# Product-key attention: SyncE fetches three sets of rows a head by byte offset instead of two by row number

## What is computed

```python
kv_scores, indices = _pk(x, Wq_pk, pk_keys)              # 16 scores and row numbers of each token and head
ind = indices + offsets[None, None, :, None]             # + head * 16384
k = jnp.einsum('bnhk,bnhkd->bnhd', kv_scores, keys_table[ind])
v = jnp.einsum('bnhk,bnhkd->bnhd', kv_scores, values_table[ind])
# causal attention of q over k, v within a head, then @ Wo, summed over the heads
```

## Time and profile before

| | us |
|---|---|
| median of three runs | 10244.51 |
| lowest, highest | 10216.51, 10246.37 |
| the profiled execution | 10217.74 |
| its span, first to last instruction | 10215.9 |
| POOL busy in the span | 7665.5 (75%) |
| VectorE busy | 6964.4 (68%) |
| TensorE matmul, weight load busy | 5480.3, 4291.3 |
| ScalarE busy | 2991.9 |

### The profile page before, as it was taken

One profiled execution on the slowest core, in us unless ns is written; L12 is line 12 of the kernel. 1 busy time (PEld: TensorE's weight loads), 2 busy tenths in 40 slices (PEclk: granted clock), 3 DMA queues, 4 the chain that ended last, 5 costly groups with the idle time before them and its releaser, 6 DMA issues.

```text
span 10215.9 us, 172728 instructions
## 1 busy us (share of the span) xinstructions
PE 5480.3 (54%) x23108; PEld 4291.3 (42%) x23108; DVE 6964.4 (68%) x42588; ACT 2991.9 (29%) x9770; POOL 7665.5 (75%) x8083
## 2 busy tenths in 40 slices
PE   5655555555555555555555555555555555555555
PEld 4444444444444444444444444444444444444343
DVE  8866666666766667666666666766667676666663
ACT  4322232222322223223232222322223222222222
POOL 5777777777777777777777777777777777777776
PEclk7877777777777777777777777777777777777777
DMA  3333333333333333333333333333333333333333
GB/s 109 104 107 107 107 111 107 107 107 107 111 107 107 107 107 111 107 107 107 107 111 107 107 107 109 109 107 107 107 109 109 107 107 107 108 108 107 107 107 99
DMA packets 458936, 1097.67 MB, mean 107 GB/s; under 512 B 164737, under 2 KB 198529, under 8 KB 457793
## 3 DMA queue, kind: packets, MB, share of 16 engines
q0 software_dynamic: 387168, 1057.74, 36.0%
q1 hardware_dynamic: 70752, 31.47, 1.2%
HBM read 1084.36 MB, written 4.19 MB: 107 GB/s over the span
## 4 chain that ended last, share of the span: by engine, by line
POOL 74%; issue 24%; DVE 1%; PE 1%; POOLq 0%; DMA 0%; ACT 0%; SPq 0%; DVEq 0%; ACTq 0%
POOL ring L325 74%; DVE hot L947 0%; DMA wo<-in_Wo 0%; POOLq L340 0%; POOLq L338 0%; PE ps_w L605 0%; PE ps_o L658 0%; PE ps_s L682 0%; DVE nmax L994 0%; DVE ps_v L869 0%; POOLq L339 0%; DMA ring<-in_table,idx 0%; POOLq L336 0%; DVE sidx L895 0%; DVE left L893 0%
## 5 line engine op out<-in xcount | busy, mean ns | idle before, releaser
L325 POOL DMA_INDIRECT ring<-in_table,idx x8066 | 7664.0, 950 | 2524.4 <-issue 2457.5
L605 PE MATMUL ps_w<-ring,diag 128*128 128x256 f32 x8192 | 2987.0, 544 | 4103.0 <-DMA ring<-in_table,idx 4103.0
L605 PEld LDWEIGHTS ps_w<-ring,diag 128*128 128x128 f32 x8192 | 2298.2, 288 | 4688.3 <-issue 4101.3
L947 DVE SCALAR_TENSOR_TENSOR hot<-rank,posf,cand 128x54 f32<-128x54 f32 x8192 | 1661.0, 272 | 0.3
L866 DVE TENSOR_SCALAR ps_v<-ring,wgt 128x256 f32<-128x256 f32 x512 | 248.8, 486 | 1928.4 <-DMA ring<-in_table,idx 1928.4
L869 DVE SCALAR_TENSOR_TENSOR ps_v<-ring,wgt,ps_v 128x256 f32<-128x256 f32 x3072 | 1478.3, 481 | 19.6
L432 ACT COPY probT<-ps_p 128x512 f32<-128x512 f32 (+3 forms) x768 | 342.4, 480 | 3909.5 <-PE ps_p L649 3897.4
L415 ACT ACTIVATE diag<-ident,wgt 128x128 f32<-128x128 f32 x4096 | 1253.3, 395 | 1.9 <-PE ps_w L605 1.9
L424 ACT ACTIVATE prob<-ps_s,nmax 128x128 f32<-128x128 f32 (+7 forms) x512 | 378.9, 740 | 2000.3 <-DVE nmax L994 2000.3
L880 DVE TENSOR_TENSOR kv<-part,ps_w 128x256 f32<-128x256 f32 x512 | 215.8, 422 | 841.6 <-PE ps_w L605 500.7
L947 DVE DVE_READ_ACCUMULATOR hot<-rank,posf,cand 128x1 f32 x8192 | 661.8, 81 | 0.0
(11 more groups left out here) (118 smaller groups left out, 7016.7 us busy)
## 6 DMA issues: line engine op xcount, KB each, us to landing
far<-in_table SPq DMA_DIRECT2D x16128, 1.0 KB
ring<-in_table,idx POOLq DMA_INDIRECT x8066
xin<-in_x SPq DMA_DIRECT2D x8, 512.0 KB, 4.6
mask<-in_adj SPq DMA_DIRECT2D x1, 4096.0 KB, 14.5
out_x<-acc SPq DMA_DIRECT2D x64, 64.0 KB
far_idx<-idx SPq DMA_DIRECT2D x126, 0.5 KB
ring<-in_WqpkT SPq DMA_DIRECT2D x1, 512.0 KB, 16.5
ring<-in_keysT SPq DMA_DIRECT2D x1, 512.0 KB, 18.5
```

The source lines that it names most:

```text
L325: pool.indirect_dma_start(out=ring[:, t % RING, k, :], out_offset=None, in_=table, in_offset=bass.IndirectOffsetOnAxis(ap=idx[:, t, k:k + ...
L605: ins = nc.tensor.matmul(pw_ps, diag[:, k, :], ring[:, t % RING, k, :], start=(k == 0), stop=(k == PE_ROWS - 1))
L947: c = step(nc.vector.scalar_tensor_tensor(out=hot[:, k, :], in0=rank[:], scalar=posf[:, k:k + 1], in1=cand[:, 1, :], op0=ALU.is_equal, op1 ...
```

## The change

`FAR` becomes (2, 5, 7): three sets a head are fetched by SP, and POOL issues 125 gathers a head instead of 126. `SETS` is another name for the same tuple.

VectorE multiplies the row number of set 15 by 1024, as a float, in the units of `FAR`, and writes the byte offset into a column of its own (`far_at`). SP copies these offsets (to `far_row`) instead of the row numbers, and its fetch addresses the table as one run of bytes, so that the value in the register is the offset itself.

The function `far_rows` is split. `far_begin` waits for `idx_ready` and issues the copy; `far_fetch` waits for the copy and for `rows_summed`, loads the values and issues the fetches. `far_sets` calls `far_begin` of the next set ahead of `far_fetch` of the present one. Each set has a semaphore of its own for the copy. At a turn between batches the stores stand behind the first two sets of the new head, not behind the first.

```diff
-FAR = (3, 7)
+FAR = (2, 5, 7)
+SETS = FAR
+        far_at = sb("far_at", [P, len(SETS)], U32)
+        far_row = sb("far_row", [1, len(SETS), P], U32)
+        table_bytes = table.bitcast(U8).rearrange("r d -> (r d)")
-            def far_rows(n, i):
-
-                t = FAR[i]
-                sp.wait_ge(idx_ready, n * UNITS + t + 1)
+            def far_begin(n, i):
+
+                sp.wait_ge(idx_ready, n * UNITS + FAR[i] + 1)
                 sp.sem_inc(sp_mark, 1)
-                    sp.dma_start(far_idx[0:1, i, :], idx[:, t, FAR_ROW:FAR_ROW + 1]).then_inc(far_idx_dma, 16)
-                sp.wait_ge(far_idx_dma, ((n - 1) * len(FAR) + i + 1) * 16)
+                    sp.dma_start(far_row[0:1, i, :], far_at[:, i:i + 1]).then_inc(far_row_dma[i], 16)
+
+            def far_fetch(n, i):
+
+                sp.wait_ge(far_row_dma[i], n * 16)
                 sp.sem_inc(sp_mark, 1)
-                sp.wait_ge(rows_summed, (n - 1) * UNITS + t + 1)
+                sp.wait_ge(rows_summed, (n - 1) * UNITS + FAR[i] + 1)
                 sp.sem_inc(sp_mark, 1)
                 for q in range(0, P, LOADED):
-                    _, rows = nc.values_load_multi_w_load_instructions(
-                        far_idx[0:1, i, q:q + LOADED], engines=[mybir.EngineType.SP],
-                        min_val=0, max_val=HEADS * NUM_KV - 1,
+                    _, at = nc.values_load_multi_w_load_instructions(
+                        far_row[0:1, i, q:q + LOADED], engines=[mybir.EngineType.SP],
+                        min_val=0, max_val=(HEADS * NUM_KV - 1) * KV_BYTES,
                     for j in range(LOADED):
-                        sp.dma_start(far[q + j:q + j + 1, i, :], table[bass.ds(rows[j], 1), :]) \
+                        sp.dma_start(far[q + j:q + j + 1, i, :].bitcast(U8), table_bytes[bass.ds(at[j], KV_BYTES)]) \
                             .then_inc(far_dma[i], 16)
+            def far_sets(n, sets, final=False):
+                for i in sets:
+                    if i < last_set:
+                        far_begin(n, i + 1)
+                    elif not final:
+                        far_begin(n + 1, 0)
+                    far_fetch(n, i)
             def turn(b):
-                far_rows((b + 1) * HEADS, 0)
+                far_sets((b + 1) * HEADS, range(0, last_set))
                 stores(b)
-                for i in range(1, len(FAR)):
-                    far_rows((b + 1) * HEADS, i)
+                far_sets((b + 1) * HEADS, range(last_set, last_set + 1))
             load(1)
+            far_begin(1, 0)
...
                 after(c)
+                if t in SETS:
+                    i = SETS.index(t)
+                    step(nc.vector.tensor_scalar(far_at[:, i:i + 1], idxf[:, FAR_ROW:FAR_ROW + 1], float(KV_BYTES), None,
+                                                 ALU.mult))
                 nc.vector.tensor_copy(idx[:, t, :], idxf[:]).then_inc(idx_ready, 1)
```

More of the change, by code:

```diff
@@ L11 @@
 U32 = mybir.dt.uint32
+U8 = mybir.dt.uint8
 AX_X = mybir.AxisListType.X
@@ L22 @@
 KV = 2 * P
+KV_BYTES = 4 * KV
 RING = 4
@@ L107, in gat_and_product_key_attention @@
         ring = sb("ring", [P, RING, TOPK, KV])
-        far = sb("far", [P, len(FAR), KV])
-        far_idx = sb("far_idx", [1, len(FAR), P], U32)
+        far = sb("far", [P, len(SETS), KV])
+        far_at = sb("far_at", [P, len(SETS)], U32)
+        far_row = sb("far_row", [1, len(SETS), P], U32)
         part = sb("part", [P, KV])
@@ L144, in gat_and_product_key_attention @@
         rows_dma = [sem(f"rows_dma{t}") for t in range(UNITS)]
-        far_idx_dma = sem("far_idx_dma")
-        far_dma = [sem(f"far_dma{t}") for t in FAR]
+        far_row_dma = [sem(f"far_row_dma{t}") for t in SETS]
+        far_dma = [sem(f"far_dma{t}") for t in SETS]
         consts = sem("consts")
@@ L208, in gat_and_product_key_attention @@
         dve_mark = sem("dve_mark")
+        table_bytes = table.bitcast(U8).rearrange("r d -> (r d)")
         def gathered(n, t):
-            return n * (TOPK - (t in FAR)) * 16 + TOPK * 16
+            return n * (TOPK - (t in SETS)) * 16 + TOPK * 16
         HALVES = [1 + (t >= 4) for t in range(TILES)]
@@ L262, in load @@
                     .then_inc(x_dma, 16)
-            def far_rows(n, i):
-                t = FAR[i]
-                sp.wait_ge(idx_ready, n * UNITS + t + 1)
+            def far_begin(n, i):
+                sp.wait_ge(idx_ready, n * UNITS + FAR[i] + 1)
                 sp.sem_inc(sp_mark, 1)
-                with nc.allow_non_contiguous_dma(reason="one row number of each token"):
-                    sp.dma_start(far_idx[0:1, i, :], idx[:, t, FAR_ROW:FAR_ROW + 1]).then_inc(far_idx_dma, 16)
-                sp.wait_ge(far_idx_dma, ((n - 1) * len(FAR) + i + 1) * 16)
+                with nc.allow_non_contiguous_dma(reason="one table address of each token"):
+                    sp.dma_start(far_row[0:1, i, :], far_at[:, i:i + 1]).then_inc(far_row_dma[i], 16)
@@ L279, in far_rows @@
                         skip_runtime_bounds_check_because="made of two positions below 128 and a head below 8")
                     for j in range(LOADED):
-                        sp.dma_start(far[q + j:q + j + 1, i, :], table[bass.ds(rows[j], 1), :]) \
+                        sp.dma_start(far[q + j:q + j + 1, i, :].bitcast(U8), table_bytes[bass.ds(at[j], KV_BYTES)]) \
                             .then_inc(far_dma[i], 16)
-            def far_all(n):
-                for i in range(len(FAR)):
-                    far_rows(n, i)
+            last_set = len(FAR) - 1
@@ L294, in _ @@
             load(1)
+            far_begin(1, 0)
             with sp.Fori(1, HEADS) as h:
-                far_all(h)
+                far_sets(h, range(len(FAR)))
             with sp.Fori(0, BATCH - 2) as b:
@@ L300, in _ @@
                 with sp.Fori(1, HEADS) as h:
-                    far_all((b + 1) * HEADS + h)
+                    far_sets((b + 1) * HEADS + h, range(len(FAR)))
             turn(BATCH - 2)
-            with sp.Fori(1, HEADS) as h:
-                far_all((BATCH - 1) * HEADS + h)
+            with sp.Fori(1, HEADS - 1) as h:
+                far_sets((BATCH - 1) * HEADS + h, range(len(FAR)))
+            far_sets(BATCH * HEADS - 1, range(len(FAR)), True)
             stores(BATCH - 1)
@@ L323, in gathers @@
             def gathers(t, first=False):
-                for k in range(TOPK if first or t not in FAR else FAR_ROW):
+                for k in range(TOPK if first or t not in SETS else FAR_ROW):
                     pool.indirect_dma_start(
@@ L860, in add_row @@
                 rows = ring[:, t % RING, k, :]
[L861 to L864, removed]
+                if k == FAR_ROW and t in SETS and not (isinstance(n, int) and n == 0):
+                    rows = far[:, SETS.index(t), :]
+                    dve.wait_ge(far_dma[SETS.index(t)], P * 16)
+                    dve.sem_clear(far_dma[SETS.index(t)])
                 if k == PE_ROWS:
```

## The result

The changed kernel takes 10212.72 us (median of 7 runs, 10211.05 to 10213.66), the kernel before in the same series 10244.67 (10216.51 to 10247.89). The ratio is 0.997, with a 95% interval of 0.996 to 0.998. In two later series the kernel before took 10217.5 and 10216.5, and in the second of them the changed one 10212.27: ratio 0.9996, 0.9986 to 1.0006. The kernel before has two levels: it took 10216.51 once and 10,244 to 10,248 six times in the series of the result, and 10245.69 in one of 18 executions of the last series. So the gain is 0 to 0.3%, depending on which of them it shows. I had forecast 10,449.

What follows compares the result with a forecast made beforehand. POOL bounds the kernel; after the change SP does, at 53.4 us a set. First fetches at 260.6, 189 sets 10,092.6, stores 68.9, x loads 3.6, then landing, tail and 1.8 us around the span: 10,449, range 10,335 to 10,565.

Steps and rivals of the forecast that it cites:

- POOL's 1.255 us a gather: POOL's indirect gathers: each takes 1.255 us, busy time and issue gap together, issued back to back.
- the floor forecast at 10,139: The run's time if POOL stays the bound: 63 gathers fewer save 79 us.
- The waits named as falling away: SP's queue: copy wait (2.0 us a set) covered by fetches; waits for idx, y_added and xn gone once SP is late.
- The MOVE stayed: SP's row fetch: the 29 ns MOVE ahead of each DMA was assumed kept, since it goes with a register-held address.
- The early copy: SP's offset copy issued one set ahead: its wait, 2.0 us a set, is hidden by a whole set's fetches.
- the sum of SP's queue: SP's queue from first fetch at 260.6 us: 189 sets of 53.4 us, stores and x loads, giving 10,449; chance 0.60.
- I take it with one gap of three, 76 ns.: SP's row fetch: dropping the register operation saves its 37 ns and one gap of 39, 9.7 us a set.
- SP's 65.3 us between two sets inside a turn: SP's time from one set to the next when late, before the change; two sets need 131 of 158 us.
- seven blocks of stores between batches, 9.64 + 0.2 us each: SP's stores at the turns between batches: 68.9 us added to SP's queue.
- A head period near 160: Sign that SP is the bound: three sets need 160.2 us a head, against 156.9 for POOL.
- the 3 us a head that POOL was to wait for kv: Sign that SP is the bound: POOL waits for kv (rows_summed) some 3 us a head.
- Rival 2: SP's set at 52.0 to 52.3 us gives 10,187 to 10,248; or DMA engines set POOL's pace, 10,218; chance 0.05.

Runs made afterwards that it cites:

- e2_row_numbers_again: The changed kernel with row numbers in place of byte offsets, so SP's fetch multiplies again; third set and early copy kept: 12380.41 us in one run.
- e5_hint: The changed kernel with a prefetch hint (hint_back_edge) for the branches that close SP's loops: 10141.32 us.
- e3_copy_with_its_set: The changed kernel with the copy of the offsets begun just before its own set; three sets and byte offsets kept: 10482.48 us, ratio 1.0258.
- e4_short_set: The changed kernel with unit 5's last 32 rows replaced by the table's first 32, fetched in one DMA: 10144.8 us, ratio 0.9928.

## Why the prediction was wrong

**Right: what bounds the kernel, and where the bound goes.** POOL's 1.255 us a gather held to 0.1%: the floor forecast at 10,139 was measured at 10144.8 and 10141.32. SP became the bound. The waits named as falling away (copy, idx, y_added) fell away: in the changed kernel SP's queue has five such waits in all. The MOVE stayed and the byte DMA took 225 ns, as assumed. The early copy was worth 1.65 us a set where 2.0 was said.

**Wrong: the sum of SP's queue, 10,449 against 10,213.66 for the profiled execution, by three terms.**
1. *"I take it with one gap of three, 76 ns."* This term was sized too small. It was 87 by the fetches' period and 90 by undoing it (e2_row_numbers_again). 14 ns a row are 1.8 us a set, and a set came to 51.6 us in place of 53.4: 189 x 1.8 = 340 us less. A gap between queue instructions isn't shared out evenly. In the medians of the two traces a register operation starts 276 ns after the start of the DMA ahead of it, a MOVE 261 ns, so removing the former took more than itself and its own gap.
2. *Not in the sum: the branch at the end of a head.* 52 taken branches make 138 us more. I had taken SP's 65.3 us between two sets inside a turn, where no such branch stands, and had put all the idle time of the other heads down to the wait for idx. e5_hint showed the term by taking most of it away.
3. *"seven blocks of stores between batches, 9.64 + 0.2 us each"*. That row held 4.0 us of wait for y_added, which the text itself said would fall away. Without waits six blocks take 5.31 us each [the timeline after] and the seventh 3.85: 31 us less, with the short gaps around them counted.

-340 + 138 - 31 = -233, and 235 was the difference; the other two lie behind the last fetch. With the first term right and nothing else changed, the sum would have been 10,109, below POOL's floor, so the omitted branch mattered as much for what bounds the kernel. A head needs 3 x 51.6 + 2.65 = 157.4 us on SP, and 156.9 on POOL. It is a near tie, in which SP pays in addition for starting at 261 us, POOL at 58, and for its stores. That puts the end 71 us above POOL's floor, and by chance within 5 us of the kernel before's.

**The signs.** The register operation gone, the wait for the copy gone, no idx wait between sets and VectorE idle before part<-far came as named. A head period near 160 did not: it was 157.4. Nor did the 3 us a head that POOL was to wait for kv: it waited 13.8 us in the whole run. At half a microsecond a head SP falls behind POOL too slowly to hold it often; the end comes late because SP's own queue ends late. Where SP needs more, in e3_copy_with_its_set with some 161 us a head, POOL's trace does show a pause of 4.5 to 5 us in most heads.

**The chances.** Rival 2 ("landing between, no difference") was priced at 52.0 to 52.3 us a set, stores and loads of x apart; counted so, with the branches spread over the sets, the changed kernel has 52.3 (10,192.1 - 261.0 - 43 for stores and loads of x, over 189). By the sum of the forecast that would still be some 10,245; the stores, 31 us less, bring it to the 10,213 that was measured. I gave it 0.05. (At 52.3 us the forecast's own sum gives 10,241, not the 10,248 printed beside it; nothing hangs on that.) The window is 0.3 us of a set, or 57 us, wide and lies 1.1 us under a price that I had called uncertain by 0.6; the uncertainty was too small, since a wrong gap of 14 ns a row alone is 1.8 us a set, and whole terms (the branch) weren't in it. The second half of rival 2, that the DMA engines set POOL's pace, is refuted by e5_hint: with as many packets and bytes on both queues as the changed kernel (384144 and 95952 packets), POOL's 8003 gathers ended the run at 10,141.

The Trainium skill (DMA: Bandwidth & Descriptors, Issuing engines are not separate DMA queues) says that issuing from another engine saves initiating time only. That is what the runs show: of the 79 us of POOL's issue time 73 and 76 were had in e4_short_set and e5_hint, once SP's own time to initiate didn't take them back.

## What to carry to other kernels

Before moving work to a queue that looks idle, add up that queue for a whole loop iteration, its loop branch included, and compare it with the iteration of the engine that is relieved: here 157.4 against 156.9 us decided between 0.7% and nothing. An instruction on such a queue costs its period, not its duration (90 ns against 37 here), and the period is only known by taking it out or putting it in. SP's loop over one head, some 800 instructions, pays 2.4 to 3.2 us at each plain branch back to its start; a hint for the target brought that to 0.6, but did nothing for the loop around it.

## What the runs showed of the hardware

- A register operation of 37 ns ahead of each fetch costs 90 ns of SP's queue (63.1 against 51.6 us for 128 fetches with their loads and copy).
- A taken branch that closes SP's loop of one head leaves 2.4 to 3.2 us before the next instruction (2.65 in the mean of 52), and 0.6 us with a prefetch hint. At the end of the loop over batches, which holds a turn and the loop over heads, the pause stays at 2.4 to 2.9 us with the hint (5 branches of e5_hint).
- A load of 16 values into SP's registers takes 1.23 us, one of 32 takes 2.12. The Trainium skill (DMA: Bandwidth & Descriptors, Latency and other measured facts) gives a floor of about 600 ns. The two sizes here point to a fixed part of 0.33 us and 0.056 us a value, which would put a load of one value below that floor; this is an estimate, and no run here has one.
- On the chip of one series all kernels took 60 to 75% longer, in timed and profiled executions alike, with unchanged median durations and late or stretched single instructions on the queues. There the changed kernel, which gives SP more instructions to issue, was 9% slower than the kernel before.
